# A perceiver block on one core: keys of 14 half batches by combined blocks, values as whole tiles, scores and weighted values two slots later

## The chip, the cores and the metric

One core of a Trainium2 chip runs the whole program. TensorE multiplies matrices into PSUM (8 banks of 512 f32 a partition), VectorE (DVE), ScalarE (ACT) and GpSimd (POOL) work elementwise, and SyncE (SP) issues transfers, transposes by DMA among them; POOL has no part in anything that lies in PSUM here. The engines run side by side and wait on semaphores. The metric is the device time in microseconds, the median of several executions.

## The reference

```python
def xattn(x, context, Wq, Wk, Wv, Wo, bo):          # 8 batches, 128 tokens of 512, context 2048 x 384
    q, k, v = x @ Wq, context @ Wk, context @ Wv     # 8 heads of 64
    sim = einsum('bihd,bjhd->bhij', q, k) * 64 ** -0.5
    return einsum('bhij,bjhd->bihd', softmax(sim), v) @ Wo + bo
x = x + xattn(layernorm(x), ctx_768, ...)
x = x + attn(layernorm(x), ...)    # causal, softmax over axis 1, with biases
x = x + ffn(layernorm(x), ...)     # 2048 hidden, relu, rounded to 8 bits
```

Nearly all the time is in the first line: keys and values of 8 x 2048 context rows.

## The kernel before

**Precision.** Each f32 operand is kept as a high and a low half in f16 (`_h`, `_l`; high by ScalarE, low = value minus high by VectorE or POOL), and a product is three passes: high x high, low x high, high x low (`three_passes`). So one block of keys, 128 features x 512 context rows with 384 summed, is 9 matmuls (3 passes, 3 pieces of 128).

**Slots.** The first stage is a loop over 128 slots, 16 a batch, 8 a half batch (1024 context rows). Slot s makes a key block (a pair p of heads, a quarter q of the rows; `key_quarter` into bank `k_ps`), a value step (`value_tiles`, two row tiles of 128 for half of the features, 2 x 9 matmuls of 256 columns into `v_ps`), and handles one head of one half batch: its scores (128 tokens x 1024 rows), its exponentials and its weighted values. Two heads of a pair, slots 2u and 2u+1, get their scores together (`scores(u)`, into banks `e_ps0` and `e_ps1`, 12 matmuls). A slot whose number modulo 16 is 8 or more is "behind": it works on the second half of its batch, so it has to join its maximum (`new_max`), its `fade` and its sum with those of the first half.

**Lags.** TensorE's slot s holds value step s+1, key block s, weighted values of slot s-5 (`PV_LAG`), and in even s the scores of unit s/2-1. VectorE takes the two maxima in the next odd slot. ScalarE (`steady`) takes the exponentials of slot s-3 (`X_LAG`) twice: `p_h` in f16, `p_f` in f32 with its sum. POOL makes `p_l` = `p_f` - `p_h` (`p_low`), SP transposes `p_h` and `p_l` by DMA to `pt_h` and `pt_l`, and TensorE waits for both in `weighted_values`, which uses banks `o_ps0` and `o_ps1` in turn; VectorE adds the result to `acc` (`accumulate`). Each engine's order is written out in code, and a wait holds up everything behind it on its engine.

**Beside it.** Once in four slots a quarter of the context (128 x 1536) is loaded into `raw` (2 buffers), its high half made by ScalarE (`ctx_high`), its low half by POOL (`ctx_low`). In slots whose number modulo 16 is 15, 1, 3 or 5, after a behind pair is done, POOL norms the output of a pair (`o_norm`, four instructions). In the last 16 slots the weights of later stages are split and turned. After the slots come projections, the second attention and the hidden layers (last, from about 750 us).

## Time and profile before

| what | value |
| --- | --- |
| median of 3 runs | 923.07 us (923.06 to 923.19) |
| the profiled execution | 923.73 us, of these 921.7 us from its first to its last instruction |
| granted clock of TensorE, mean | 0.997 |
| the 128 slots | from about 28 to about 715 us |
| TensorE busy | 905.2 us (98%) |
| VectorE, ScalarE, POOL busy | 548.3, 576.5, 507.4 us (59, 63, 55%) |

Matmuls overlap in the pipe, so the distance from one start to the next tells what one costs, not its own duration. A granted clock of 1.00 is the 2.4 GHz level. Idle time of an engine that nothing waits for costs nothing.

### The profile page before, as it was taken

How to read it: one execution, taken by the hardware profiler on the slowest of the kernel's cores; microseconds unless marked ns; L12 is line 12 of the kernel's file. 1: busy time of each engine (PE TensorE's matmuls, PEld its weight loads, DVE VectorE, ACT ScalarE, POOL GpSimd, SP SyncE). 2: the span in 40 equal slices, each digit the busy share in tenths (PEclk: the TensorE clock that was granted, in tenths of full speed). 3: DMA queues.
4: the chain of work that ended last, by engine and by line, in shares of the span. 5: the costliest groups of instructions: out<-in, count | busy, mean ns of one | idle time of the engine just before them, and what ended most of it. 6: DMA issues, size and time to landing. Idle time of an engine off the chain costs nothing.

```text
span 921.7 us, 19492 instructions
## 1 busy us (share of the span) xinstructions
PE 905.2 (98%) x7470; PEld 565.6 (61%) x7470; DVE 548.3 (59%) x973; ACT 576.5 (63%) x1014; POOL 507.4 (55%) x393
## 2 busy tenths in 40 slices
PE   7999999999999999999999999999999899999998
PEld 4556666666666666666666666666666455544444
DVE  6645565555555555655555565556667669886633
ACT  4756777776677777777776677777567423236540
POOL 4636567556555755675576556778876755310000
PEclk9999999999999999999999999999999999999999
DMA  9377576676657566565666666857997462223502
GB/s 339 84 150 161 138 132 136 159 142 144 144 132 139 127 144 142 128 143 140 139 153 144 143 138 141 198 132 149 182 189 157 92 127 70 71 85 74 183 12 81
DMA packets 340267, 126.35 MB, mean 137 GB/s; under 512 B 316112, under 2 KB 317904, under 8 KB 340176
## 3 DMA queue, kind: packets, MB, share of 16 engines
q1 hardware_dynamic: 324832, 95.87, 49.4%
q10 hardware_dynamic: 15344, 29.23, 10.6%
q8 instruction: 61, 1.00, 0.5%
q14 instruction: 30, 0.25, 0.1%
HBM read 45.36 MB, written 2.10 MB: 51 GB/s over the span
## 4 chain that ended last, share of the span: by engine, by line
PE 94%; ACT 2%; DVE 1%; DMA 1%; issue 1%; SPq 1%; ACTq 0%; DVEq 0%
PE v_ps L670 28%; PE k_ps L670 27%; PE e_ps L739 10%; PE e_ps L670 8%; PE o_ps L759 6%; PE o_ps L761 3%; PE e_ps L1021 3%; PE o_ps L776 2%; PE o_ps L1014 1%; PE e_ps L1014 1%; PE o_ps L954 1%; PE v_ps L1014 1%; SPq L636 1%; DMA raw<-in_ctx_t 1%; PE k_ps L1014 0%
## 5 line engine op out<-in xcount | busy, mean ns | idle before, releaser
L1979 POOL TENSOR_TENSOR p_l<-p_f,p_h 128x1024 f16<-128x1024 f32 x128 | 273.1, 2134 | 233.4 <-ACT p_f L1202 233.4
L1537 DVE TENSOR_REDUCE q_max<-e_ps 128x1 f32<-128x1024 f32 x128 | 153.4, 1219 | 48.9 <-PE e_ps L739 48.9
L1530 DVE TENSOR_TENSOR k_l<-k_ps,k_h 128x512 f16<-128x512 f32 x128 | 88.5, 691 | 126.3 <-ACT k_h L1166 126.3
L1523 DVE TENSOR_TENSOR v<-v_ps,v 128x512 f16<-128x512 f32 x127 | 87.8, 691 | 112.5 <-ACT v L1158 112.5
L1195 ACT ACTIVATE p_h<-e_ps,bias 128x1024 f16<-128x1024 f32 x128 | 143.3, 1120 | 2.4 <-issue 0.3
L1202 ACT ACTIVATE p_f<-e_ps,bias 128x1024 f32<-128x1024 f32 x128 | 142.1, 1111 | 0.0
L670 PE MATMUL v_ps<-wv_h,ctx_h 128*128 128x256 f16 x756 | 124.4, 273 | 1.7 <-DVE v L1523 1.7
L670 PE MATMUL v_ps<-wv_l,ctx_h 128*128 128x256 f16 x756 | 123.7, 273 | 0.0
L670 PE MATMUL v_ps<-wv_h,ctx_l 128*128 128x256 f16 x756 | 123.7, 273 | 0.0
L759 PE MATMUL o_ps<-v,pt_h 128*128 128x128 f16 x1024 | 104.2, 220 | 0.7 <-DVE acc L1554 0.7
L670 PE MATMUL k_ps<-ctx_h,wk_h 128*128 128x512 f16 x384 | 103.8, 379 | 0.0
L670 PE MATMUL k_ps<-ctx_h,wk_l 128*128 128x512 f16 x384 | 103.8, 379 | 0.0
L670 PE MATMUL k_ps<-ctx_l,wk_h 128*128 128x512 f16 x384 | 103.8, 379 | 0.0
L1969 POOL TENSOR_TENSOR ctx_l<-raw,ctx_h 128x1536 f16<-128x1536 f32 x31 | 96.1, 3099 | 13.4 <-ACT ctx_h L1145 11.7
L761 PE MATMUL o_ps<-v,pt_l 128*128 128x64 f16 x1024 | 100.8, 193 | 0.0
L759 PEld LDWEIGHTS o_ps<-v,pt_h 128*128 128x128 f16 x1024 | 90.3, 98 | 15.8 <-issue 0.9
L1158 ACT ACTIVATE v<-v_ps 128x512 f16<-128x512 f32 x127 | 75.0, 590 | 37.0 <-PE v_ps L670 35.0
L761 PEld LDWEIGHTS o_ps<-v,pt_l 128*128 128x128 f16 x1024 | 88.6, 98 | 15.0
L1166 ACT ACTIVATE k_h<-k_ps 128x512 f16<-128x512 f32 x128 | 76.6, 598 | 15.9 <-PE k_ps L670 15.7
L670 PEld LDWEIGHTS v_ps<-wv_h,ctx_h 128*128 128x128 f16 x756 | 64.6, 98 | 34.7 <-issue 28.5
L670 PEld LDWEIGHTS v_ps<-wv_h,ctx_l 128*128 128x128 f16 x756 | 74.0, 98 | 8.6
L670 PEld LDWEIGHTS v_ps<-wv_l,ctx_h 128*128 128x128 f16 x756 | 74.0, 98 | 8.6
(311 smaller groups left out, 1286.9 us busy)
## 6 DMA issues: line engine op xcount, KB each, us to landing
raw<-in_ctx_t ACTq DMA_DIRECT2D x27, 768.0 KB, 5.5
w_raw<-in_w_t SPq DMA_DIRECT2D x32, 256.0 KB, 4.0
raw<-in_ctx_t SPq DMA_DIRECT2D x4, 768.0 KB, 7.5
pt_h<-p_h SPq DMA_TRANSPOSE x128, 2.8
pt_l<-p_l SPq DMA_TRANSPOSE x128, 2.8
out<-xr SPq DMA_DIRECT2D x7, 256.0 KB, 2.0
x_in<-in_x SPq DMA_DIRECT2D x6, 256.0 KB, 8.4
o_all<-in_x ACTq DMA_DIRECT2D x6, 256.0 KB, 3.7
```

The source lines that it names most:

```text
L670: mm = pe.matmul(acc, a(c), m(c), start=(i == 0), stop=(i == len(todo) - 1))
L739: mm = pe.matmul(e_ps[h][:, i, :], left[rows, p, tokens], right[rows, u % K_RING, cols], start=first, stop=last)
L759: pe.matmul(acc_bank[:, 0:VW], pt_h[:, s % T_RING, j, :], v[g][:, tile, head, :], start=(j == 0), stop=False, skip_group_check=True)
L761: mm = pe.matmul(acc_bank[:, 0:DH], pt_l[:, s % T_RING, j, :], v[g][:, tile, head, 0:DH], start=False, stop=(j == 2 * JT - 1), skip_group_ ...
L1166: act.activation(k_h[:, u % K_RING, i * QW:i * QW + QW], k_ps[:, :], ACT.Copy).then_inc(k_hi, 1)
L1195: act.activation(p_h[:, s % H_RING, :, :], e_ps[s % 2][:, :, :], ACT.Exp, scale=EXP_SCALE, bias=bias[:, col:col + 1]).then_inc(p_hi, 1)
L1202: act.activation(p_f[:, s % F_RING, :, :], e_ps[s % 2][:, :, :], ACT.Exp, scale=EXP_SCALE, bias=bias[:, col:col + 1], accum_out=p_sum[:, c ...
L1523: dve.tensor_tensor(v[g][:, j0:j0 + 2, :, DH:VW], v_bank(s)[:, :].rearrange("p (j h d) -> p j h d", j=2, d=DH), v[g][:, j0:j0 + 2, :, 0:DH ...
L1530: dve.tensor_tensor(k_l[:, s // 2 % K_RING, cols], k_ps[:, :], k_h[:, s // 2 % K_RING, cols], ALU.subtract)\
L1537: ins = dve.tensor_reduce(q_max[:, col:col + 1], e_ps[s % 2][:, :, :].rearrange("p i n -> p (i n)"), AX, ALU.max, negate=True)
L1969: pool.tensor_tensor(ctx_l[b % 2][:, q, :, :], raw[:, i % 2, :, :], ctx_h[b % 2][:, q, :, :], ALU.subtract).then_inc(ctx_split, 1)
L1979: pool.tensor_tensor(p_l[:, s % L_RING, :, :], p_f[:, s % F_RING, :, :], p_h[:, s % H_RING, :, :], ALU.subtract).then_inc(p_split, 1)
```

## The change

**Keys.** For the half batches 1 to 14 (`mixed(s)`: slots 8 to 119) four slots make the four key blocks of two feature blocks and two quarters together. Of the three pieces of the sum, two form a 2 x 2 by 2 x 2 product of blocks, which is done with 7 products (Strassen) for 8; the third piece is added in plain. That is 33 matmuls of 512 columns for 36. The combined weights are made once (`key_weights` on POOL, `wk_high`, `wk_low`, 10 forms in `wf_h`, `wf_l`). The combined context blocks T1 to T4 are made once a half batch: POOL forms them in place in `raw` (`mix_ctx`, four instructions of 128x512), ScalarE their high halves (`mix_high`, two of 128x1024), POOL their low halves (`mix_low`, two). Sums of products that serve two results are copied by VectorE from PSUM to `kept` (`keep_product`, three a round of four slots) and added to a bank, into bank `s_ps` (`add_keys`, three a round); then ScalarE and VectorE split as before. `s_ps` is the bank that was `o_ps1` in the slots, so weighted values have `o_ps0` alone.

**Values.** From slot 8 on, a value step is one tile of 128 rows for all 512 features: 9 matmuls of 512 columns for 18 of 256.

**Order.** `X_LAG` 3 to 5, `PV_LAG` 5 to 7, scores of unit s/2-2 in even slots. In a round's slots 0 and 2 the weighted values stand first. Both quarters of a half batch's context are handled in its predecessor's slots 1 and 2 (modulo 8), mixes in 3 and 4, their splits in 5 and 6; `raw` has 3 buffers, the key ring 3 in place of 4. The work on the weights, the loads of x and the order after the slots are rewritten to fit. `bv_row` is loaded after the slots.

```diff
+        X_LAG, PV_LAG = 5, 7
...
+            return (s // 4, 2 * (s % 4), 2) if s < PER_HALF else (None, s % PER_BATCH, 1)
...
+                ctx_behind[at - 7], ctx_behind[at - 6] = 2 * hb, 2 * hb + 1
+                mix_behind[at - 5], mix_behind[at - 4] = (hb, 0), (hb, 1)
+                mixed_behind[at - 3], mixed_behind[at - 2] = (hb, 1), (hb, 0)
...
+            def key_product(s, acc, first, *terms):
...
+                key_product(s, s_ps, True, ("A12", (1, 0)), ("W0", (2, 0)))
...
+                key_product(s, k_ps, True, ("A11", (0, 0)))
+
+            def sixth_product(s):
+                pe.wait_ge(k_added, 3 * group_of(s) + 1)
+                pe.wait_ge(mix_split, mixed_at(s // PER_HALF, 0))
+                key_product(s, k_ps, False, ("S2", "T2"))
+
+            def fifth_product(s):
+                pe.wait_ge(k_split, split_at(group_of(s), 1))
+                key_product(s, s_ps, True, ("S1", "T1"), ("W1", (2, 1)))
+
+            def third_products(s):
+                pe.wait_ge(k_kept, 3 * group_of(s) + 3)
+                key_product(s, s_ps, False, ("S4", (1, 1)), ("WD", (2, 1)))
+                key_product(s, k_ps, False, ("S3", "T3"))
+
+            def fourth_product(s):
+                pe.wait_ge(k_added, 3 * group_of(s) + 3)
+                key_product(s, k_ps, False, ("A22", "T4"), ("W1", (2, 0)))
...
-                if s >= 2:
-                    pe.wait_ge(acc_ready, s - 1)
-                elif s == 0:
+                if s:
+                    pe.wait_ge(acc_ready, s)
+                else:
                     pe.wait_ge(q_split, 8)
-                acc_bank, head = o_ps[s % 2], 2 * (p % 2) + h
+                acc_bank, head = o_ps0, 2 * (p % 2) + h
...
+                j = s % 4 if mixed(s) else None
+                if j in (0, 2):
+                    weighted_values(s - PV_LAG)
                 if s + 1 < SLOTS:
                     value_tiles(s + 1)
...
+                elif j == 0:
+                    first_products(s)
+                elif j == 1:
+                    sixth_product(s)
                     weighted_values(s - PV_LAG)
+                    fifth_product(s)
+                elif j == 2:
+                    third_products(s)
+                else:
+                    weighted_values(s - PV_LAG)
+                    fourth_product(s)
+                if s % 2 == 0 and s >= 4:
+                    scores(s // 2 - 2)
...
+            weighted_values(SLOTS - 7)
+            scores(UNITS - 2)
+            fold(0)
+            weighted_values(SLOTS - 6)
+            project_out(0)
+            weighted_values(SLOTS - 5)
+            project_out(1)
             scores(UNITS - 1)
...
+                elif j == 0:
+                    v_high(s + 1)
+                    key_high(s, "C11")
+                elif j == 2:
+                    v_high(s + 1)
+                    key_high(s, "C12")
+                elif j == 3:
+                    key_high(s, "C21")
...
+                dve.tensor_copy(kept_sum[:, place_at, :], bank[:, :]).then_inc(k_kept, 1)
...
+                dve.tensor_tensor(s_ps[:, :], bank[:, :], other, ALU.add).then_inc(k_added, 1)
...
+                    keep_product(s, 2)
+                    keep_product(s, 3)
+                elif j == 2:
+                    gather(done)
+                    v_low(s + 1)
+                    add_keys(s, "C12")
+                    key_low(group_of(s), "C12")
+                    add_keys(s, "C22")
+                else:
+                    maxima(s)
+                    gather(done)
+                    v_low(s + 1)
+                    key_low(group_of(s), "C22")
...
+                    pool.tensor_tensor(left[:, 0, :], right[:, 0, :], left[:, 0, :], ALU.subtract).then_inc(mix_ready, 1)
...
                 if s in ctx_behind:
                     ctx_low(ctx_behind[s])
+                if s in mix_behind:
+                    mix_ctx(*mix_behind[s])
+                if s in mixed_behind:
+                    mix_low(*mixed_behind[s])
```

How the order changes on two engines. POOL, in the slots where an output is normed too (o_sum to o_half is `o_norm`, p_l a slot each, ctx_l a quarter of the context), before:

```order
L1995 TENSOR_TENSOR o_half<-o_f,o_half 128x128
L1979 TENSOR_TENSOR p_l<-p_f,p_h 128x1024
L1969 TENSOR_TENSOR ctx_l_87<-raw,ctx_h_86 128x1536
L1979 TENSOR_TENSOR p_l<-p_f,p_h 128x1024
L1986 TENSOR_TENSOR o_sum<-acc 128x128
L1989 TENSOR_TENSOR o_f<-o_sum,o_rec 128x128
L1993 CAST o_half<-o_f 128x128
L1995 TENSOR_TENSOR o_half<-o_f,o_half 128x128
L1979 TENSOR_TENSOR p_l<-p_f,p_h 128x1024 x2
```

POOL after the change, from slot 1 of an even half batch (raw<-raw is a mix):

```order
L2246 TENSOR_TENSOR ctx_l_93<-raw,ctx_h_92 128x1536
L2287 TENSOR_TENSOR p_l<-p_f,p_h 128x1024
L2246 TENSOR_TENSOR ctx_l_93<-raw,ctx_h_92 128x1536
L2287 TENSOR_TENSOR p_l<-p_f,p_h 128x1024
L2294 TENSOR_TENSOR o_sum<-acc 128x128
L2297 TENSOR_TENSOR o_f<-o_sum,o_rec 128x128
L2301 CAST o_half<-o_f 128x128
L2303 TENSOR_TENSOR o_half<-o_f,o_half 128x128
L2254 TENSOR_TENSOR raw<-raw 128x512
L2255 TENSOR_TENSOR raw<-raw 128x512
L2287 TENSOR_TENSOR p_l<-p_f,p_h 128x1024
L2258 TENSOR_TENSOR raw<-raw 128x512
```

The two ctx_l of a half batch now have one p_l between them, and mixes follow where there was p_l alone. VectorE, around the maxima (q_max) of a pair, before:

```order
L1537 TENSOR_REDUCE q_max<-e_ps 128x1 x2
L1566 TENSOR_SCALAR o_den<-p_sum,fade 128x1
L1554 SCALAR_TENSOR_TENSOR acc<-acc,fade,o_ps 128x128
L1571 RECIPROCAL o_rec<-o_den 128x2
L1523 TENSOR_TENSOR v_103<-v_ps,v_103 128x8x64
L1530 TENSOR_TENSOR k_l<-k_ps,k_h 128x512
```

And after, from the middle of slot 2 of a round to slot 3 (m_ps holds the banks k_ps and s_ps):

```order
L1761 TENSOR_TENSOR m_ps<-m_ps,kept 128x512
L1736 TENSOR_TENSOR k_l<-m_ps,k_h 128x512
L1761 TENSOR_TENSOR m_ps<-m_ps,kept 128x512
L1767 TENSOR_REDUCE q_max<-e_ps 128x1
L1772 TENSOR_SCALAR new_max<-q_max 128x1
L1767 TENSOR_REDUCE q_max<-e_ps 128x1
L1772 TENSOR_SCALAR new_max<-q_max 128x1
L1796 TENSOR_SCALAR o_den<-p_sum,fade 128x1
L1784 SCALAR_TENSOR_TENSOR acc<-acc,fade,o_ps 128x128
L1721 TENSOR_TENSOR v<-v_ps,v 128x2x4x64
```

Two sums and a low half of keys now stand ahead of the maxima, and the accumulation behind them.

## Rows read from the trace of the kernel before

**Rows 1.** The page: busy us, share of the span, instructions.
```profile
PE 905.2 (98%) x7470; PEld 565.6 (61%) x7470; DVE 548.3 (59%) x973; ACT 576.5 (63%) x1014; POOL 507.4 (55%) x393
```

**Rows 2.** Busy time by stretch: stretch, length, then PE, PEld, DVE, ACT, POOL, granted clock, DMA.
```profile
100.00:700.00 600.00, 600.00 (x5512) 402.57 (x5509) 344.71 (x601) 427.88 (x755) 388.47 (x270) 1.00 0.68 146
```

**Rows 3.** Timeline of TensorE: start, us, line, operation, out<-in, shapes, count.
```profile
303.40 0.39 PE L739 MATMUL e_ps<-k_h,q_h 64*128 64x512 f16 x2
...
304.80 0.50 PE L670 MATMUL v_ps<-wv_h,ctx_h 128*128 128x256 f16 x3
...
306.77 0.81 PE L670 MATMUL k_ps<-ctx_h,wk_h 128*128 128x512 f16 x3
307.42 0.81 PE L670 MATMUL k_ps<-ctx_h,wk_l 128*128 128x512 f16 x3
...
308.72 0.22 PE L759 MATMUL o_ps<-v,pt_h 128*128 128x128 f16 x1
...
309.40 0.49 PE L670 MATMUL v_ps<-wv_h,ctx_h 128*128 128x256 f16 x3
```

**Rows 4.** Timeline of POOL; in brackets idle before and who ended it.
```profile
301.06 0.45 POOL L1986 TENSOR_TENSOR o_sum<-acc 128x128 f32<-128x128 f32 x1
...
302.81 2.13 POOL L1979 TENSOR_TENSOR p_l<-p_f,p_h 128x1024 f16<-128x1024 f32 x1
...
309.27 2.13 POOL L1979 TENSOR_TENSOR p_l<-p_f,p_h 128x1024 f16<-128x1024 f32 x1 [1.12 <-ACT p_f L1202]
...
319.95 2.13 POOL L1979 TENSOR_TENSOR p_l<-p_f,p_h 128x1024 f16<-128x1024 f32 x1 [4.49 <-ACT p_f L1202]
```

**Rows 5.** Groups of POOL: busy us, mean ns; last, the landing of pt_l.
```profile
L1979 POOL TENSOR_TENSOR p_l<-p_f,p_h 128x1024 f16<-128x1024 f32 x128 | 273.1, 2134 | 233.4 <-ACT p_f L1202 233.4
L1969 POOL TENSOR_TENSOR ctx_l<-raw,ctx_h 128x1536 f16<-128x1536 f32 x31 | 96.1, 3099 | 13.4 <-ACT ctx_h L1145 11.7
...
L2075 POOL TENSOR_TENSOR xr<-xr,o_all 128x512 f32<-128x512 f32 x8 | 12.1, 1548 | 0.0
...
L2025 POOL TENSOR_TENSOR o_all<-o_all,bo_row 128x512 f32<-128x512 f32 x6 | 7.5, 1268 | 0.0
...
DMA to landing us min/median/max: 2.7/2.8/6.7
```

**Rows 6.** Timeline of all engines: rows of VectorE and ScalarE.
```profile
299.42 0.69 DVE L1530 TENSOR_TENSOR k_l<-k_ps,k_h 128x512 f16<-128x512 f32 x1 [0.89 <-ACT k_h L1166]
...
300.02 0.26 DVE L1566 TENSOR_SCALAR o_den<-p_sum,fade 128x1 f32<-128x1 f32 x1
...
300.21 0.33 DVE L1554 SCALAR_TENSOR_TENSOR acc<-acc,fade,o_ps 128x128 f32<-128x128 f32 x1
...
304.91 2.35 DVE L1537 TENSOR_REDUCE q_max<-e_ps 128x1 f32<-128x1024 f32 x2 [0.77 <-PE e_ps L739]
...
307.51 0.59 ACT L1158 ACTIVATE v<-v_ps 128x512 f16<-128x512 f32 x1
...
307.99 1.12 ACT L1202 ACTIVATE p_f<-e_ps,bias 128x1024 f32<-128x1024 f32 x1
```

**Rows 7.** Groups of ScalarE and VectorE: busy us, mean ns.
```profile
L1145 ACT ACTIVATE ctx_h<-raw 128x1536 f16<-128x1536 f32 x31 | 45.7, 1474 | 0.0
...
L1542 DVE TENSOR_SCALAR new_max<-q_max 128x1 f32<-128x1 f32 x64 | 13.7, 214 | 2.3
```

**Rows 8.** Timeline of TensorE after the last slot.
```profile
709.32 0.39 PE L739 MATMUL e_ps<-k_h,q_h 64*128 64x512 f16 x2
...
714.27 0.22 PE L759 MATMUL o_ps<-v,pt_h 128*128 128x128 f16 x1 [0.75 <-DVE acc L1554]
...
717.93 0.39 PE L739 MATMUL e_ps<-k_h,q_h 64*128 64x512 f16 x2 [2.82 <-ACT p_f L1202]
```

**Rows 9.** Busy time by stretch, there.
```profile
720.00:721.00 1.00, 1.00 (x4) 0.34 (x3) 0.96 (x3) 0.00 (x0) 1.00 (x1) 0.50 2.03 88
```

**Rows 10.** The chain of waits there: start, us, what.
```profile
719.57 4.17 PE v_ps L670 x12
```

More of the change, by code:

```diff
@@ L436, in made_bank @@
             return t_bank[(made.index(item) + 2) % 4]
[L438 removed]
+        fold_bank = [s_ps, s_ps, t_bank[0], t_bank[1]]
         def norm_at(what, r):
@@ new lines, in key_quarter @@
+                three_passes(k_ps[:, :], (lambda c: wh[c], lambda c: wl[c]),
+                             (lambda c: ch[:, q % 2, c, :], lambda c: cl[:, q % 2, c, :]), CC).then_inc(k_filled, 1)
+            def key_product(s, acc, first, *terms):
+                hb, c2 = s // PER_HALF, s % PER_HALF // 4
+                for part, (wi, xi) in enumerate(((0, 0), (1, 0), (0, 1))):
+                    for t, (name, block_of) in enumerate(terms):
+                        w = (wf_h, wf_l)[wi][:, FORMS.index(name), c2, :]
+                        if block_of in MIXES:
+                            x = (mix_h, mix_l)[xi][hb % 2][:, MIXES.index(block_of), :]
+                        else:
+                            x = (ctx_h, ctx_l)[xi][hb % 2][:, block_of[1], block_of[0], :]
+                        mm = pe.matmul(acc[:, :], w, x, start=(first and part == 0 and t == 0),
+                                       stop=(part == 2 and t == len(terms) - 1), skip_group_check=True)
+                mm.then_inc(k_filled, 1)
@@ L1214, in _ @@
             k_high(0)
-            wk_high(slice(P, D))
+            for n in range(1, 4):
+                wk_high(n)
             ctx_high(1)
@@ L1549, in accumulate @@
                 dve.wait_ge(pv_done, s + 1)
-                new, total = o_ps[s % 2][:, 0:VW], acc[:, p, h, :]
+                new, total = o_ps0[:, 0:VW], acc[:, p, h, :]
                 if half:
@@ L1600, in _, with gather, maxima @@
                 q_low(i)
-            def steady(s):
-                done = s - PV_LAG - 1
-                if s % 2 == 1 and 0 <= s - X_LAG < SLOTS:
+            def gather(done):
+                if behind(done):
+                    add_sums(done)
+                accumulate(done)
+                if stage_end(done) is not None:
+                    o_reciprocal(stage_end(done))
+            def maxima(s):
+                slot_maximum(s - X_LAG)
+                slot_maximum(s - X_LAG + 1)
@@ L1606, in steady @@
                     slot_maximum(s - X_LAG)
+                    key_low(group_of(s), "C11")
                     slot_maximum(s - X_LAG + 1)
[L1609 to L1618 removed]
```

553 lines of the change are left out of this document (365 added, 188 removed).

## Prediction, made before the changed kernel ran

> **What bounds the kernel now.** I read first the busy time of each engine over the whole span, and the same in the stretch from 100 to 700 us [rows 1, 2]. TensorE is busy 905.2 of 921.7 us, and for all 600.00 us of that stretch, at a granted clock of 1.00 (the 2.4 GHz level). So in the slots TensorE sets the pace, and a saving there is worth its full size until another engine fails to deliver in time. POOL (GpSimd) is busy 388.47 of those 600 us, VectorE 344.71, ScalarE 427.88: there is room on average.
>
> Then the timeline of TensorE over one pair of slots [rows 3]: scores take 303.40 to 304.80, a value step (18 matmuls of 256 columns) to 306.77, so 1.97 us, a key step (9 of 512 columns) to 308.72, so 1.95 us, 0.65 per three, and weighted values to 309.40, 0.68 us. POOL's p_l instructions of even slots start at 309.27 and 319.95 [rows 4]: two slots last 10.68 us, four 21.36, a half batch (8 slots) 42.72.
>
> **What TensorE saves.** In each of 28 rounds of four slots the keys need 33 matmuls for 36: three fewer, 0.65 us. A whole value tile is 9 matmuls of 512 columns, by the key step's spacing 9 x 0.216 = 1.94 against 1.97, so 0.03 a slot, 0.1 a round. A round becomes 21.36 - 0.75 = 20.6 us, a half batch 41.2. Over 28 rounds that is 21.0 us; the 8 plain slots at the end add 0.2. Unhindered the median 923.1 would become 901.9.
>
> The TensorE page of the Trainium skill ("TensorE: Matmul & The Clock Gate", Back-to-back issue gap) gives a sustained spacing of 131 ns for 512 columns, beside 2.5 ns plus the columns for an isolated one. By the sustained figure the whole tiles alone would take 9 x 0.131 = 1.18 us a slot and some 90 us would go. The trace does not agree: matmuls of just this shape, back to back, are 0.216 apart [rows 3].
>
> **A round after the change, on TensorE's own clock** (0 = start of the round, no waits; 0.1 between scores and their neighbours). Slot 0: weighted values 0 to 0.7, value 2.6, two products into s_ps 3.9, one into k_ps 4.6, scores 4.7 to 6.0. Slot 1: value 6.1 to 8.0, sixth product 8.7, weighted values 9.3, fifth 10.6. Slot 2: weighted values 11.3, value 13.3, third products 14.6 (s_ps) and 15.2, scores 15.3 to 16.6. Slot 3: value 16.7 to 18.6, weighted values 19.3, fourth 20.6. Two things now stand at a slot's start that stood at its end: the weighted values of slots 0 and 2. They need (a) the transpose of p_l and (b), since there is one bank o_ps0 for two, VectorE's accumulation of the step before.
>
> **What is added elsewhere.** POOL, per half batch: four mixes of 128x512 in f32, no such row. The nearest are 1.27 us for o_all with bo_row and 1.55 for xr with o_all [rows 5]; I take 1.30, as the first is the nearest in kind (both inputs large, VectorE busy beside it); ends 1.2 and 1.55. Two low halves of 128x1024, 2.1 us each by p_l. Together 9.4 us. VectorE, per round: three copies out of a bank and three sums of a bank and SBUF, 128x512; k_l of the same size takes 0.69 with 0.60 from start to start [rows 6], so 3.9 us; VectorE stood at 57% of 21.36, so 12.3, and comes to 16.2 of 20.6 (79%). ScalarE: two of 128x1024 a half batch, 1.0 each (two thirds of ctx_h's 1.47 [rows 7]). Loads of the context stay 768 KB each, with three buffers for two: I cost them at nothing.
>
> The GPSIMD page of the skill ("GPSIMD Engine Reference", The C++ chunk loop) states a floor of about 2.5 cycles an element for two inputs. Worked out at its clock that would be an estimated 1.07 us for a mix; the sum below would then be some 6 us lower in all. The rows of 128x512 stand above it [rows 5].
>
> **POOL in the even half batches.** There every second slot also has o_norm, four instructions, 301.06 to 302.81 = 1.75 us [rows 4]. Averages hide the place: count from the scores of slot 0 in a half. VectorE's first maximum starts 1.51 after scores start (303.40, 304.91 [rows 3, 6]), so at 6.2. These slots also take new_max (0.21 and about 0.04 for the wait [rows 7]), and key_low of C11 (0.60) lies between the maxima: 6.2 + 1.18 + 0.25 + 0.60 + 1.18 + 0.25 = 9.65, p_f starts at 9.85 and p_l can start 1.28 later (307.99, 309.27 [rows 4, 6]), at 11.1. From there POOL has without a pause: p_l of slots 1 to 6, 6 x 2.09 = 12.5; o_norm of 1, 3, 5, 5.25; two ctx_l, 6.2 [rows 5]; four mixes, 5.2; the first mix_low, 2.1: 31.3 us. Its last p_l ends at 42.4, and its transpose lands 2.7 later [rows 5], at 45.2. TensorE wants it at 41.2. Each p_f is ready before POOL gets to it (the tightest, slot 5, by 0.8). So an even half lasts about 45.2: TensorE waits 4.0 us in it. By intermediate sums the waits are 2.4 us at slot 4 (p_l of slot 2 starts at 18.1, behind o_norm and ctx_l, instead of 14.8; lands 23.0, wanted 20.6), 1.0 at slot 6, 0.6 at the end. Before, the same p_l landed with ample time: weighted values stood at the end of the second slot behind it.
>
> **VectorE in the odd half batches.** No o_norm there, so POOL delivers within about 0.2. But the end of a round is a chain: in slot 1 p_f, fade and mix_high end on ScalarE at 12.1, p_h, p_f and v of slot 2 at 14.8 (p_f takes 1.12 and p_h has its size, each about 1.05 to the next start, v 0.6 [rows 6]); v_low 15.4; sum C12 16.1; its high half 16.75, low half 17.5; sum C22 18.2; two maxima with new_max 21.0; then o_den and acc, 0.53 [rows 6]: 21.5, where the next weighted values want it at 20.6. That is 1.0 in the second round; in the first round (ctx_high 1.47, but no new_max nor fade) 0.2. Odd halves: 41.2 + 1.2 = 42.4. In the even halves the same chain would cost 1.5 at slot 4, hidden under POOL's 2.4.
>
> **The sum.** Even halves 45.2 - 42.7 = +2.5, seven of them +17.5; odd ones 42.4 - 42.7 = -0.3, seven -2.1; plain slots -0.2. The tail: the last scores wait for p_f now, 8.6 us after the scores before them (709.32, 717.93), with 0.75 and 2.82 us of idle [rows 8] and a granted clock of 0.50 behind it [rows 9]. After the change the last but one wait so, and the last have cover: 1.3 of scores, three sets of 12 matmuls (2.6 each) and two weighted values, 10.5 us. The start, with scores a slot pair later, may lose an early wait. I take 0 for both, ends -4 and +3. Profiled span 921.7 + 15.2 = 936.9; what lies around it (923.73 - 921.7 = 2.0) stays; the median is 0.7 below the profiled execution: 923.1 + 15.2 = **938.3 us**.
>
> **Rivals.** (1) *TensorE stays the bound*: POOL's chain lags less than its rows say, or the p_l order gives enough room. Against it: 31.3 us of POOL work, for which 41.2 - 11.1 - 2.7 = 27.4 are there. For it: latencies are tenths, and all depends on differences. With a fifth to nothing of the waits it gives 902 to 909; with half, 920. Faster, 0.25. (2) *The clock falls*: the idle of 2.4 us at slot 4 of even halves could do what the tail shows, where 0.75 and 2.82 us of idle with 0.7 of work between them brought a granted clock of 0.50 (the 1.2 GHz level) [rows 8, 9]. Each time costs about 1.6 us (twelve matmuls in 4.17 [rows 10], for 12 x 0.216 = 2.6), seven 11: 949. It decides only if 2.4 us of idle suffice, which no row shows. 0.15. (3) *ScalarE and VectorE become the bound everywhere*: p_f of slot 0 is ready 0.4 before scores want it (25.3); if the sums into a bank cost 0.3 more each, every round is 0.6 longer: 28 x 0.6 on top, 955. 0.08. (4) *Nothing to tell*: waits just eat the 21 us, 923. 0.05. The forecast itself, waits of 28 to 45 us in all, has 0.47: 930 to 947.
>
> **Chances and range.** This kernel can be told from no change at 0.2% (1.8 us). Faster 0.25 (rival 1), same 0.05 (rival 4), slower 0.70. The mix price moves 7 x 4 x 0.25 = 7 us, p_f of slot 1 another 3, the tail 4. From 908 to 950 no more than 2 in 10 is left out (the best part of rival 1, rival 3 and the worst of rival 2).
>
> **What would show it.** TensorE idle before weighted values (o_ps<-v,pt_h), some 35 us in all where there is 0.7 now, released by a DMA (pt_l) in even half batches and by VectorE's acc in odd ones; key and value rows near 0.216 a matmul; POOL without a gap from the second to the seventh slot of an even half and a mix at 1.3 us; even half batches of 45, odd ones of 42.4. Wrong at the first step, if TensorE is still 99% busy in the slots; wrong at the POOL step, if its waits in both kinds of half are alike; at the chain step, if scores wait for p_f; rival 2, if the granted clock falls in the middle.

## The result, and the profile after

| | before | after |
|---|---|---|
| median of the runs, us | 923.13 (923.06 to 923.42) | 985.63 (982.33 to 987.2) |
| profiled execution, us | 923.73 | 985.50 |
| its span, us | 921.7 | 983.7 |
| scores of slot 8 start at, us | 79.1 | 85.1 |
| from there to the scores of slot 120 | 598.2 | 634.5 |
| from there to the end | 244.4 | 264.0 |

The ratio is 1.0672, interval 1.0644 to 1.0699: 6.7% slower. Slower was forecast, but at 938.3 us, with a range that ended at 950. The three last lines of the table share out the 62 us: 6.0 at the start, 36.3 in the slots, 19.6 in the tail. The forecast was 0, 15.4 (less 0.2 in the plain slots) and 0. The two ends are not quite like for like: slot 8 now has the scores of a unit earlier, so one set of scores and two weighted values, by [rows 3] an estimated 2.8 us of TensorE's work, have passed from the start to the tail. With that counted back the start lost 8.8 us and the tail 16.8.

The page of the changed kernel, as in [rows 1]: TensorE has 1164 matmuls less (6306 for 7470), is busy as long as before and has a lower share of a longer span.
```profile
PE 907.9 (92%) x6306; PEld 448.8 (46%) x6306; DVE 653.3 (66%) x1143; ACT 602.4 (61%) x1046; POOL 639.8 (65%) x482
```
The stretch of [rows 2], the same columns: TensorE 560.37 of 600 us in place of all of it, at a granted clock of 0.98 on average.
```profile
100.00:700.00 600.00, 560.37 (x4141) 273.51 (x4140) 408.14 (x719) 430.24 (x743) 470.03 (x321) 0.98 0.62 136
```
What TensorE waited for from 85 to 720 us (line, who released it, us in all, times, the longest). Before, this view has no row for the slots.
```profile
PE o_ps L902 <- issue: 23.3, 14, 2.9
PE o_ps L902 <- DMA pt_l<-p_l: 14.9, 7, 2.2
PE o_ps L902 <- DVE acc L1784: 1.3, 8, 0.2
PE v_ps L764 <- DVE v L1721: 1.0, 1, 1.0
```
40.5 us, nearly all before weighted values, as forecast (some 35). But few of them are released by VectorE. "issue" means that the view names no releaser; these stand at slot 6 of a half batch (one at slot 2). The trace can still tell what they are. Each of the 14 ends 0.09 us behind the landing of a pt_l, that is the start of the transpose plus its time to landing. For the wait that ends at 202.69 (a row shown below) the one transpose issued between 196 and 200 us is
```profile
L681 SPq DMA_TRANSPOSE pt_l<-p_l x1: 1233/1233/1233, 197.5 to 197.5; - x1
...
DMA to landing us min/median/max: 5.1/5.1/5.1
```
so TensorE waits here for a transpose that is slow to land; the experiment with the load tells why it is slow.

POOL's groups of the changed kernel, for [rows 5]:
```profile
L2287 POOL TENSOR_TENSOR p_l<-p_f,p_h 128x1024 f16<-128x1024 f32 x128 | 273.9, 2140 | 133.1 <-ACT p_f L1384 130.3 <-DMA pt_l<-p_l 2.4
L2246 POOL TENSOR_TENSOR ctx_l<-raw,ctx_h 128x1536 f16<-128x1536 f32 x31 | 96.1, 3100 | 12.8 <-ACT ctx_h L1309 12.7
L2265 POOL TENSOR_TENSOR mix_l<-raw,mix_h 128x1024 f16<-128x1024 f32 x28 | 60.1, 2145 | 21.9 <-ACT mix_h L1316 21.9
L2258 POOL TENSOR_TENSOR raw<-raw 128x512 f32<-128x512 f32 x14 | 17.8, 1268 | 0.1
```
The mix costs 1.27 us where 1.30 was taken, its low half 2.15 where 2.1 was.

A half batch took 42.7 us before. After, from scores to scores: even ones 44.9, 44.9, 47.7, 47.7, 44.9, 45.0, 47.4 (forecast 45.2), odd ones 43.2, 46.0, 43.9, 43.2, 43.3, 45.9, 46.4 (forecast 42.4). So the even ones that nothing else disturbed came as forecast, and the excess is in the odd ones and in single halves of 46 and more. These hold the second surprise, the clock. TensorE behind one of the longer idles, and then two stretches there (columns as in [rows 2]):
```profile
202.69 0.26 PE L902 MATMUL o_ps<-v,pt_h 128*128 128x128 f16 x1 [2.41 <-issue]
203.94 1.47 PE L764 MATMUL v_ps<-wv_h,ctx_h 128*128 128x512 f16 x3
```
```profile
202.00:204.00 2.00, 1.31 (x17) 1.34 (x18) 0.00 (x0) 1.66 (x3) 2.00 (x2) 0.66 0.59 116
204.00:206.00 2.00, 2.00 (x7) 0.66 (x6) 0.29 (x1) 0.00 (x0) 2.00 (x2) 0.50 0.98 223
```
After an idle of 2.41 us three matmuls take 1.47 us from first to last end where 0.81 was usual [rows 3], at the 1.2 GHz level. Six such falls lie between slots 8 and 120, near 203, 340, 418, 566, 657 and 691 us. Busy time times what was missing of the clock, summed over stretches of 2 us, is 9.2 us, 1.5 each; rival 2 had put 1.6 on one. The same sum gives 4.0 us between 20 us and the scores of slot 8 (falls near 66 and 76 us) and 4.4 from slot 120 on, where the kernel before has 0 and 1.7. So some 16 of the 62 us are lost clock, 4.0 of them at the start and 2.7 in the tail.

### The profile page after: what moved, and what is told of

Its sections match the earlier page's. It is cut to its first block, busy times and chain, and to the rows that moved or that the text cites. A ratio compares the mean times of both kernels' runs of the same rounds, so it can differ in the third digit from the quotient of the medians.

```text
span 983.7 us, 17461 instructions
## 1 busy us (share of the span) xinstructions
PE 907.9 (92%) x6306; PEld 448.8 (46%) x6306; DVE 653.3 (66%) x1143; ACT 602.4 (61%) x1046; POOL 639.8 (65%) x482
## 3 DMA queue, kind: packets, MB, share of 16 engines
q1 hardware_dynamic: 324432, 95.09, 44.9%
## 4 chain that ended last, share of the span: by engine, by line
PE 71%; DVE 9%; issue 6%; POOL 6%; ACT 4%; DMA 3%; SPq 1%; ACTq 0%; DVEq 0%; POOLq 0%
PE v_ps L764 21%; PE m_ps L832 15%; PE e_ps L764 7%; PE e_ps L882 6%; PE o_ps L902 5%; DVE q_max L1767 4%; PE m_ps L764 3%; PE e_ps L1176 3%; POOL p_l L2287 3%; PE o_ps L904 2%; DMA pt_l<-p_l 2%; POOL ctx_l L2246 2%; PE e_ps L1169 1%; DVE m_ps L1761 1%; PE m_ps L1169 1%
## 5 line engine op out<-in xcount | busy, mean ns | idle before, releaser
L1348 ACT ACTIVATE k_h<-m_ps 128x512 f16<-128x512 f32 x112 | 66.7, 596 | 108.5 <-DVE m_ps L1761 108.4
L764 PE MATMUL v_ps<-wv_h,ctx_h 128*128 128x512 f16 (+1 forms) x396 | 108.1, 383 | 1.5 <-DVE v L1721 1.5
L764 PE MATMUL v_ps<-wv_h,ctx_l 128*128 128x512 f16 (+1 forms) x396 | 106.9, 380 | 0.0
L764 PE MATMUL v_ps<-wv_l,ctx_h 128*128 128x512 f16 (+1 forms) x396 | 104.7, 374 | 0.0
L2246 POOL TENSOR_TENSOR ctx_l<-raw,ctx_h 128x1536 f16<-128x1536 f32 x31 | 96.1, 3100 | 12.8 <-ACT ctx_h L1309 12.7
L1736 DVE TENSOR_TENSOR k_l<-m_ps,k_h 128x512 f16<-128x512 f32 x112 | 76.8, 686 | 36.1 <-ACT k_h L1348 36.1
L1743 DVE COPY kept<-m_ps 128x512 f32<-128x512 f32 x84 | 55.2, 685 | 56.0 <-PE m_ps L832 56.0
L2265 POOL TENSOR_TENSOR mix_l<-raw,mix_h 128x1024 f16<-128x1024 f32 x28 | 60.1, 2145 | 21.9 <-ACT mix_h L1316 21.9
L832 PE MATMUL m_ps<-ctx_h,wf_h 128*128 128x512 f16 x196 | 65.4, 380 | 0.0
L832 PE MATMUL m_ps<-ctx_l,wf_h 128*128 128x512 f16 x196 | 65.2, 379 | 0.0
L832 PE MATMUL m_ps<-ctx_h,wf_l 128*128 128x512 f16 x196 | 65.1, 379 | 0.0
```

Of the source, the lines that this page charges most:

```text
L764: mm = pe.matmul(acc, a(c), m(c), start=(i == 0), stop=(i == len(todo) - 1))
L832: mm = pe.matmul(acc[:, :], w, x, start=(first and part == 0 and t == 0), stop=(part == 2 and t == len(terms) - 1), skip_group_check=True)
L1736: dve.tensor_tensor(k_l[:, u, cols], src[:, :], k_h[:, u, cols], ALU.subtract).then_inc(k_split, 1)
L2246: pool.tensor_tensor(ctx_l[hb % 2][:, i % 2, :, :], raw_of(i), ctx_h[hb % 2][:, i % 2, :, :], ALU.subtract).then_inc(ctx_split, 1)
```

## Experiments

All twelve kernels are variants of the changed one. The times from scores to scores are read from TensorE's timeline, each from the one profiled execution of its kernel; how much they scatter was not measured.

| kernel | median us | ratio to before (interval) | slots 8 to 120 | to the end |
|---|---|---|---|---|
| changed kernel | 985.6 | 1.0672 (1.0644 to 1.0699) | 634.5 | 264.0 |
| e1_load_late | 970.4 | 1.0512 (1.048 to 1.0543) | 621.0 | 264.4 |
| e2_norm_late | 979.0 | 1.0603 (1.0587 to 1.0619) | 629.4 | 262.1 |
| e3_tail_spread | 988.8 | 1.0726 (1.0695 to 1.0756) | 633.6 | 265.0 |
| e4_plain_keys | 945.0 | 1.0232 (1.0217 to 1.0247) | 598.4 | 264.8 |
| e5_ends | 979.8 | 1.056 (1.0483 to 1.0637) | 640.0 | 254.8 |
| e6_middle | 960.9 | 1.0422 (1.0371 to 1.0474) | 611.1 | 262.2 |
| e7_all | 951.2 | 1.03 (1.028 to 1.0319) | 610.4 | 257.2 |
| e8_gather | 975.6 | 1.0553 (1.0519 to 1.0587) | 627.1 | 262.2 |
| e9_keeps_short | 961.1 | 1.0412 (1.0397 to 1.0428) | 609.1 | 265.3 |
| e10_mixes_short | 968.7 | 1.0502 (1.0477 to 1.0526) | 619.7 | 262.3 |
| e11_share | 958.0 | 1.0381 (1.0351 to 1.0411) | 616.8 | 259.0 |
| e12_order | 954.3 | 1.0348 (1.0331 to 1.0365) | 614.3 | 255.4 |

**A load beside a transpose.** e1_load_late moves one DMA by one slot:
```
             if hb > 1:
-                load_behind[at - 12], load_behind[at - 9] = 2 * hb, 2 * hb + 1
+                load_behind[at - 11], load_behind[at - 9] = 2 * hb, 2 * hb + 1
```


> The changed kernel with one edit: the first context load of each half batch is issued by ScalarE one slot later (slot 5 of a half batch in place of slot 4). Theory A (the 768 KB load runs beside the transpose of p_l that the weighted values of slot 6 need, which lands after 3.8 to 5.1 us in place of 2.7): TensorE's idle of 0.9 to 2.9 us at slot 6 of the odd half batches falls below 0.4, some 12 us in all, and the falls of the granted clock behind the idles of 2.4 us and more go with it, 2 to 3 us each for three or four of them: 963 to 970 us. Theory B (VectorE's or POOL's chain is late there and the load only stands beside it): nothing moves, 984 to 987. Theory C (the load now meets another needed transpose): the idle moves to slot 0 of the next half batch and the time stays within 3 us.

Measured 970.4, 15.2 less. The changed kernel has this at slot 4 of a first (odd) half batch (timeline: start, us, queue or engine; then, from the view of the tile pt_l, how long the one transpose issued from 108 to 112 us took to land):
```profile
107.23 0.37 ACTq L1415 DMA_DIRECT2D raw<-in_ctx_t  x1
...
109.12 1.23 SPq L681 DMA_TRANSPOSE pt_l<-p_l  x1
...
113.34 0.22 PE L902 MATMUL o_ps<-v,pt_h 128*128 128x128 f16 x1 [1.37 <-issue]
```
```profile
DMA to landing us min/median/max: 4.1/4.1/4.1
```
and e1_load_late, with the load a slot later (the same two views, the landing for 109 to 112 us):
```profile
110.37 1.23 SPq L681 DMA_TRANSPOSE pt_l<-p_l  x1
...
112.09 0.40 ACTq L1415 DMA_DIRECT2D raw<-in_ctx_t  x1
...
113.25 0.22 PE L902 MATMUL o_ps<-v,pt_h 128*128 128x128 f16 x1
```
```profile
DMA to landing us min/median/max: 2.8/2.8/2.8
```
(All of e1_load_late is 1.3 us later here, so its 113.25 is on time.) The transpose beside the load lands after 4.1 us and the weighted values of slot 6 start 4.2 behind its issue, after a wait; without the load it lands after 2.8 and nothing waits. Slow landings are not new: between slots 8 and 120 the kernel before has them up to 6.7 us and e4_plain_keys up to 6.5, and in neither does TensorE wait for one. There the weighted values stand at the end of a slot. The Trainium skill ("Trainium Kernel Development and Optimization", Key Constraints) says that DMAs issued from different engines' queues all run on the same 16 DMA engines and interleave; by that rule a load on ScalarE's queue can hold up a transpose on SP's, and these rows agree. Odd half batches fell to 42.1 to 42.5 us, all but one: theory A, and the forecast's 42.4 with it. The one left, 48.2, has the loads of x (slots 104 to 111) in it: TensorE waits 3.6 us for a pt_l that took 6.3 to land, and the clock falls behind that. Whether the loads of x are the cause isn't shown: e7_all, where they stand in other slots, has 42.6 there, but so has e6_middle, where they stand as here (a wait of 0.8 us).

**POOL's order.** e2_norm_late takes o_norm of batches 0 to 4 out of the slots in which it stands ahead of ctx_l (the transposes of its result stand a slot later with it):
```
+            NORM_BEHIND[PER_BATCH * b + (21 + p if b < 5 else 17 + 2 * p)] = n
...
-                done = s - PV_LAG - 1
-                if done >= 0 and stage_end(done) is not None:
-                    o_norm(stage_end(done))
...
+                if s in NORM_BEHIND:
+                    o_norm(NORM_BEHIND[s])
```


> The changed kernel with one edit: POOL's o_norm of batches 0 to 4 stands at slots 5, 6, 7 and 8 behind the batch's end in place of slots 1, 3, 5 and 7, behind the slot's other POOL work; the amount of work is the same. Theory A (POOL's order makes the p_l of the even slots late in the even half batches): their idles of 2.1 us and 1.0 at slots 4 and 6 go, five even half batches fall from 44.9 to 47.7 us to about 42, the odd ones stay: 12 us of waits and two falls of the clock at 2.7, so 966 to 972 us. Theory B (those waits come from the DMA side, loads and transposes, and not from POOL's order): 983 to 987 us.

Measured 979.0, 6.6 less. The wait at slot 4 of an even half changed its kind and size: 2.1 us for the transpose of p_l before, now
```profile
145.26 0.22 PE L907 MATMUL o_ps<-v,pt_h 128*128 128x128 f16 x1 [1.13 <-DVE acc L1789]
```
That is the VectorE wait which the prediction had at 1.5 us, hidden under POOL's 2.4. Theory A for the cause of the wait at slot 4; the time lies between the two theories. Slot 6 of the even halves went on waiting, 1.0 to 2.6 us, for transposes that met the load. TensorE was idle for no less of the slots than before, 42.2 us for 41.0; what this run gained there, 5.1 us, goes with the clock, which fell twice in place of six times. Together the two edits gave 24.7 us, where their sum is 21.8:

> The changed kernel with the edits of e1_load_late and e2_norm_late together. Alone they gave 15.2 and 6.6 us. Theory A (two causes, and in e2_norm_late the load's transfer still made slot 6 wait, now in the even half batches too): together they give more than the sum: odd half batches 42.2 us, the even ones with moved o_norm about 42.5 (1.1 of wait for VectorE's accumulation left), no fall of the clock in them; slots 8 to 120 take 602 to 608 us against 634.5, and the time is 952 to 960. Theory B (the two are independent): 963 to 965. Theory C (one cause, both take away the same waits): 968 or more.

Measured 960.9, just above theory A's 952 to 960 and below B's 963: even halves with a moved o_norm 43.3 to 43.8, odd ones 42.2 to 43.7, and no fall of the clock in them, as A had it. Its four executions lie between 958.7 and 968.3, so the 2.9 us beyond the sum are not shown by the times; the wait at slot 6 of the even halves, gone now, is what speaks for A.

**Without the combined products.** e4_plain_keys has `mixed(s)` return False and no mixes:
```
         def mixed(s):
-            return PER_HALF <= s < SLOTS - PER_HALF
+            return False
```


> The changed kernel without the combined products: the keys of all slots by 36 plain products a round, no mixes, no kept products or sums; whole value tiles, the two later slots, one bank for the weighted values, three buffers of raw context and the moved work of the tail stay. Theory A (TensorE sets the pace again as soon as POOL's mixes and VectorE's sums are gone): slots 8 to 120 at 21.26 us a round, 28 rounds 595 us against 634.5, so 39 less, with the start's 6 and the tail's 19.6 us still there: 944 to 950 us. Theory B (the later slots and the one bank cost by themselves, by waits on the accumulation): TensorE idles before weighted values of every round, over 0.2 us each, and the time is above 952. Theory C (start and tail were late because of the combined products' work too): below 940.

Measured 945.0: theory A. Its stretch from 100 to 670 us, and all that TensorE waited for from slot 8 to 120:
```profile
100.00:670.00 570.00, 568.21 (x4274) 288.82 (x4272) 324.18 (x571) 405.74 (x720) 356.46 (x247) 1.00 0.66 145
```
```profile
PE e_ps L880 <- ACT p_f L1382: 1.8, 7, 0.3
```
So the two later slots, the one bank and the whole tiles cost the slots nothing: 598.4 us against 598.2. (Two slots take 10.64 us against 10.68, the 0.02 a slot that whole tiles give; seven waits of 0.25 for p_f take back most of it.) The combined products, meant to save TensorE 21 us, cost 36.1 with the order that belongs to them: where `mixed(s)` is false the weighted values stand at the slot's end again, so this kernel doesn't tell the products from their order. The start is 79.2 us, as before the change, so the 6.0 us there come with the combined products; the tail, 264.8 us, is long without them too.

**The amounts.** Two kernels cut work out of the suspected engines.

> e6_middle with VectorE's three kept copies of a round cut to 64 of 512 columns from the second round on (so most of the keys that need them are computed from stale sums); everything else runs. Each copy is then some 0.5 us shorter, 1.5 of VectorE's round. Theory A (with loads and POOL's order mended, VectorE's chain is what keeps a round above TensorE's 20.6 us): odd half batches fall from 42.2 to 43.7 to about 41.4, even ones from 43.4 to 42 to 42.5, slots 8 to 120 from 611 to 595 to 600, 945 to 950 us in all. Theory B (POOL and the transposes set what is left): odd ones stay at 42.2 or more, 958 to 962.

Measured 961.1, the same as e6_middle: theory B by its numbers. VectorE's chain in e9_keeps_short, rows of a second round:
```profile
201.62 0.69 DVE L1767 TENSOR_TENSOR m_ps<-m_ps,kept 128x512 f32<-128x512 f32 x1
202.97 0.69 DVE L1741 TENSOR_TENSOR k_l<-m_ps,k_h 128x512 f16<-128x512 f32 x1 [0.66 <-ACT k_h L1353]
203.77 0.70 DVE L1767 TENSOR_TENSOR m_ps<-m_ps,kept 128x512 f32<-128x512 f32 x1
204.38 1.22 DVE L1773 TENSOR_REDUCE q_max<-e_ps 128x1 f32<-128x1024 f32 x1
...
205.76 1.21 DVE L1773 TENSOR_REDUCE q_max<-e_ps 128x1 f32<-128x1024 f32 x1
...
207.32 0.34 DVE L1790 SCALAR_TENSOR_TENSOR acc<-acc,fade,o_ps 128x128 f32<-128x128 f32 x1
```
The kept copies lie ahead of an idle of VectorE and are not in this chain, which begins with the third product's sum; the accumulation ends at 207.66 and a second round takes 21.49 us whether the copies are long or short. A round wants 20.63 to 20.7. So in the odd half batches it is VectorE that is late, by what stands behind the copies, and not POOL as B had it; in the even ones the second round (21.46) waits for a pt_l that landed in the usual 2.7 to 2.8 us, so there p_l itself comes late.

> e1_load_late with POOL's four mixes of a half batch cut to 64 of 512 columns (so the mixes are wrong in the other columns); o_norm stays in its old slots. POOL has some 4.3 us less in each half batch. Theory A (in the even half batches TensorE waits for POOL's 31.3 us between its second and its last p_l, as the prediction worked out): the idles of 2.1 us at slot 4 and about 1 in all behind it go, and VectorE's 1.1 to 1.5 us at slot 4, hidden till now, comes up: even half batches of 42.3 to 43 in place of 45, odd ones at 42.2 as before; slots 8 to 120 in 602 to 608 us, 951 to 958 in all. Theory B (the transposes are late for another reason than POOL's order): even ones at 44.5 or more, 967 to 971.

Measured 968.7, 1.7 less than e1_load_late: theory B by the time. But A's mechanism was only half tried. The waits, slots 8 to 120:
```profile
PE o_ps L902 <- DMA pt_l<-p_l: 15.2, 7, 2.4
PE o_ps L902 <- issue: 8.7, 9, 3.0
```
The seven waits of 2.1 us are for the p_l at slot 2, which stands behind o_norm and ctx_l and ahead of all mixes. I had overlooked in that expectation what the prediction itself says. What the mixes do delay, the p_l behind them, brought 0.5 us in an even half batch (its second round 21.47 us for 21.99); and five even half batches had a fall of the clock, four of them behind their 2.1 us, where e1_load_late had three.

**Another order on VectorE and ScalarE.**

> e1_load_late with one more edit: in each fourth slot VectorE accumulates the weighted values between the two maxima, in place of behind both. Theory A (what is left of waits in the odd half batches, 0.5 to 0.7 us a half before the weighted values of a round's first slot, is VectorE's accumulation in line behind the maxima): these waits go, seven times 0.6, 4 us: 965 to 967 against 970.4; the even half batches stay at 45. Theory B (the second maximum, 0.6 us later, makes p_f and with it p_l later): the even ones grow by about 0.6 each, the sum is the same, 969 to 972.

> e7_all without the accumulation between the maxima, and with the first kept copy of a round on ScalarE (0.6 us) in place of VectorE. Theory A (VectorE is the bound of what is left and ScalarE has room): half batches of 42 to 42.6, slots 8 to 120 in 596 to 602 us with the two late even half batches at 45, start at 80.4, 257 us from slot 120 on: 936 to 944. Theory B (ScalarE's chain from p_h to p_f is as tight; the copy makes p_f late and scores wait for it): idle before scores in each round, 950 or more.

> e7_all with the same work and another order in each mixed round: in the fourth slot VectorE does the first maximum, the accumulation, the low half of the value tile and then the second maximum (e7_all had the value's low half behind the second maximum), in the third slot ScalarE copies the value tile ahead of p_f; besides, o_norm of batches 5 and 6 is moved like that of the others. Theory A (what holds a second round at 21.5 us is the chain forecast: third product, sum C12, its high and low half, sum C22, two maxima, and whatever stands behind them, the accumulation in e6_middle, the value's low half in e7_all, in each case 0.5 to 0.7 us late): with both ahead of the second maximum the waits of 0.4 to 0.6 us at the end of a second round and for v go, a half batch is 41.5 to 42.2 us in both kinds, slots 8 to 120 take 586 to 596, the whole 925 to 938. Theory B (something behind the second maximum is late in its turn: C22's low half or p_h, and with it p_l on POOL): half batches stay at 42.5 or more, 942 to 952.

e8_gather gave 975.6, e11_share 958.0, e12_order 954.3: none is faster than the kernel it was made from (970.4, and for the last two 951.2). What TensorE waited for in the slots of e8_gather, and in those of e12_order:
```profile
PE v_ps L764 <- DVE v L1721: 6.4, 13, 1.7
```
```profile
PE o_ps L917 <- issue: 18.5, 30, 2.2
PE e_ps L897 <- ACT p_f L1399: 7.8, 15, 0.8
```
In e8_gather the waits for the accumulation are gone and 13 for v are there; odd half batches 42.6 in place of 42.2. In e12_order both are gone: scores wait for p_f in 15 places, up to 0.8 us, and the 30 waits of "issue" end, like those above, 0.09 us behind the landing of a pt_l. One of them, and the transpose issued between 151 and 153 us:
```profile
154.06 0.22 PE L917 MATMUL o_ps<-v,pt_h 128*128 128x128 f16 x1 [0.53 <-issue]
```
```profile
L694 SPq DMA_TRANSPOSE pt_l<-p_l x1: 1232/1232/1232, 151.2 to 151.2; - x1
...
DMA to landing us min/median/max: 2.7/2.7/2.7
```
18 of the 30 landed so, in 2.7 to 2.8 us, as quick as any: there p_l itself came late. In e11_share the waits for the accumulation are longer (12.8 us in 13 places; 0.96 at the end of most second rounds of odd half batches, up to 0.70 in e6_middle, where the accumulation also stands behind both maxima); ScalarE's copy is the likely cause, but e11_share also lacks e7_all's place for the accumulation. Theory B in e12_order by mechanism, at 954 against its 952; in e8_gather neither, since the time is above both and the even half batches didn't grow by 0.6 each; in e11_share a third thing, neither waits for scores nor a gain. Each order hands the 0.5 to 0.8 us of a second round to another reader. e12_order has no fall of the clock between slots 8 and 120 and is at 614.3 us there all the same.

**Start and tail.** e3_tail_spread and e5_ends:

> The changed kernel with one edit: the eight pairs of weight transposes stand one behind each of the slots 115 to 122 on SP's queue, in place of 1, 2, 1, 2, 1 and 1 behind 115, 117, 118, 119, 120 and 121. Theory A (the pairs that stand two together delay the transposes of p_h and p_l, for which TensorE waits 1.5 + 0.6 + 3.7 + 3.8 us in the last slots): 5 to 8 us less, 978 to 981. Theory B (the queue is full from 739 to 776 us whatever the order, so that the same sum is only shared out in another way): within 2 us of the changed kernel, 984 to 987.

> The changed kernel with two edits, one before slot 8 and one behind slot 112, which the trace tells apart. At the start VectorE's two low halves of the combined key weights (2.2 us each) stand behind the maxima of slot 7 in place of ahead of them. At the end the turned aq weights get a home of their own in the mixes' buffer that is idle from slot 112 on, so that their transposes start at slot 112 and not at 115 (the norms of rows 4 to 7 move to another buffer, and two sets of products change places for it). Theory A (start: TensorE waits 2.75 and 3.73 us for a chain behind these two low halves; end: the transposes of the weights, held back until the context of slot 119 is used up, fill SP's queue from 739 to 776 us and with it delay p_l): the scores of slot 8 start 3 to 4.4 us earlier, and from the scores of slot 120 to the end it takes 246 to 252 us in place of 264: 963 to 970 us in all. Theory B (the queue is as full with four slots more, and the order of folds costs as much): the end stays above 258, 978 to 983.

e3_tail_spread gave 988.8, no less than the changed kernel (the intervals overlap): theory B. SP's queue of the changed kernel shows why; this is a part of what is back to back from 739 to 776 us:
```profile
739.09 1.30 SPq L667 DMA_TRANSPOSE aq_h<-av_h  x1
740.43 1.27 SPq L667 DMA_TRANSPOSE aq_l<-av_l  x1
741.75 1.27 SPq L667 DMA_TRANSPOSE aq_h<-av_h  x1
743.05 1.90 SPq L667 DMA_TRANSPOSE aq_l<-av_l  x1
745.06 1.25 SPq L678 DMA_TRANSPOSE pt_h<-p_h  x1
746.35 1.31 SPq L681 DMA_TRANSPOSE pt_l<-p_l  x1
747.71 1.27 SPq L667 DMA_TRANSPOSE aq_h<-av_h  x1
```
Sixteen transposes of weights, 1.3 us each, have to pass with those of p, 14 of them here. What TensorE waited for from 720 us to the end, in the changed kernel, and, for e5_ends, from 723 us:
```profile
PE o_ps L902 <- issue: 6.8, 5, 3.7
PE o_ps L902 <- DMA pt_l<-p_l: 3.8, 1, 3.8
PE v_ps L764 <- DMA q_l<-o_half: 3.3, 1, 3.3
PE o_ps L902 <- DVE acc L1784: 1.6, 1, 1.6
```
```profile
PE o_ps L912 <- DVE acc L1798: 5.3, 2, 3.6
PE e_ps L774 <- DMA at_l<-n_half: 1.4, 1, 1.4
```
The main edits of e5_ends:
```
-        WEIGHT_BEHIND = {115: (0,), 117: (1, 2), 118: (3,), 119: (4, 5), 120: (6,), 121: (7,)}
+        WEIGHT_BEHIND = {112: (0,), 113: (1,), 114: (2,), 115: (3,), 117: (4,), 118: (5,), 120: (6,), 121: (7,)}
...
-                if i == 0:
-                    sp.wait_ge(k_filled, last_keys(SLOTS - PER_HALF - 1))
+                if i in (0, 4):
+                    sp.wait_ge(k_filled, last_keys(SLOTS - (1 if i else 2) * PER_HALF - 1))
...
-                elif s == 6:
-                    wk_low(4)
-                    wk_low(5)
```
(the two `wk_low` stand behind the maxima of slot 7 instead). From slot 120 on it took 254.8 us in place of 264.0, and the start 1.7 us less (4.8 in e7_all, where also the load of slot 4 is a slot later; the wait there is for the accumulation, behind VectorE's queue, 1.2 to 5.0 us in these kernels). Between A and B at both ends: the earlier home is worth 9.2 of the tail's 19.6 us, less than A had. What replaced the waits for transposes is VectorE's accumulation, 3.6 us in one place, which the single bank lets through to TensorE. The slots took 5.5 us longer than in the changed kernel. 2.5 of these lie in the last half batch (49.9 for 47.4), into which transposes of weights have moved, but e6_middle has 49.9 there without that; the rest lies in half batches that no edit of e5_ends touches. Of its four executions one took 966.4 us (mean granted clock 0.989) and three 979.4 to 981.1 (0.981 to 0.984). Waits that hang on where a load and a transpose meet, and the falls behind them, may differ so from execution to execution; with one trace it isn't shown. The times of the regions are read beside the medians for that reason, and a difference of a few us in one region is weak evidence by itself.

**All together.**

> The changed kernel with the edits of e5_ends and e6_middle, VectorE's accumulation between the two maxima of each fourth slot in place of behind them, and the loads of x in other slots (97, 99, 101, 103, 105, 107, 111, 115 for 104 to 111). Theory A (with the causes named, TensorE is the bound again): half batches of 41.3 to 42 us, two of 45 left, slots 8 to 120 in 586 to 594 us, start 81.5, from slot 120 on 246 to 252: 915 to 927 us, about the kernel before, from 2 behind it to 8 ahead. Theory B (POOL at 36 to 39 of 41 us in every half batch leaves no room, and waits come back in other slots): slots 8 to 120 stay above 600, 930 or more.

Measured 951.2: 34 us less than the changed kernel, and theory B on the slots (610.4 us). Its odd half batches take 42.5 to 43.3, the even ones 43.3 to 43.7 with two of 46.0 and 47.9. No version beats the kernel before.

## Why the prediction was right and wrong

**The first step** (TensorE's saving) held: a round without a wait takes 20.7 us (10.64 and 10.05 in e1_load_late), against 20.6, so it saves 0.67 us a round where 0.75 was counted. The 131 ns that the Trainium skill states for a matmul of 512 columns ("TensorE: Matmul & The Clock Gate", Back-to-back issue gap) have no support in the runs either: the two slots of e4_plain_keys take 10.64 us.

**The POOL step** held for what it described: 44.9 against 45.2 us an undisturbed even half batch, waits of 2.1 and 1.0 at slots 4 and 6 against 2.4 and 1.0, the first one released by the transpose of p_l, and with o_norm moved replaced by a wait of 1.1 us for VectorE. (The 1.0 was right in part by chance: without the load beside it, in e1_load_late, it is 0.6.) Mix prices of 1.27 for 1.30. The Trainium skill's floor of 2.5 cycles ("GPSIMD Engine Reference", The C++ chunk loop), which by an estimate made 1.07 us of a mix, is not reached by the mixes. By the same estimate p_l (128x1024) would take 2.13 and ctx_l (128x1536) 3.20; they take 2.14 and 3.10, so the longer instructions stand at that figure or just under it, and only the short mixes take clearly more an element.

**The VectorE chain** held, but it was hidden by something else. The forecast's 1.2 us an odd half batch, 42.4, is what e1_load_late shows in six of seven (42.1 to 42.5), with 0.5 to 0.7 of it as a wait for acc where 1.0 was forecast; that the total comes so near is in part luck, since the rounds themselves take 0.1 more than 20.6. e2_norm_late and e9_keeps_short confirm two details: 1.1 us come up at slot 4 when POOL's 2.1 go, and the kept copies are not in the chain.

**The step that failed first** is "Loads of the context stay 768 KB each ...: I cost them at nothing". Their size did stay. But the change moved the issue of the first one from slot 3 to slot 4 of a half batch and took away the slack behind the transpose that it now meets: before, a late p_l had time till the end of its slot, now weighted values stand at the slot's start. The view to ask was in the rows: the landing of pt_l, 2.7 at the least, 2.8 in the median and 6.7 at the most [rows 5]; the sum used 2.7 for every one, where the slow end of that row had become the price. Measured, the transposes before slot 6 took 3.1 to 6.1 us, and moving the load away gave 13.5 us in the slots (634.5 to 621.0) with the falls that followed.

**The second** is rival 2, left out of the forecast with 0.15: the clock did fall, six times between slots 8 and 120 at 1.5 us, 9.2 us together, against seven at 1.6. Its condition, "only if 2.4 us of idle suffice", was met by idles of 2.2 to 2.9 us, though not by all: in e1_load_late two idles of the same kind, 2.15 and 2.17 us, were followed by a clock of 0.75 and of 1.00 (stretches of 2 us behind them, columns as in [rows 2]):
```profile
234.00:236.00 2.00, 2.00 (x21) 1.16 (x22) 1.20 (x4) 2.00 (x4) 2.00 (x2) 0.75 0.42 95
147.00:149.00 2.00, 2.00 (x23) 1.23 (x22) 1.20 (x4) 2.00 (x4) 2.00 (x2) 1.00 0.33 73
```
It was no rival but an addition to the forecast's own waits.

**The third**, and by its size the largest, is "I take 0 for both, ends -4 and +3" for start and tail: 6.0 and 19.6, of the 46.9 us beyond the forecast. The tail's sum looked at TensorE's cover for the last scores, and not at SP's queue. The diff had the rows for it: the transposes of weights begin at 115 in place of 111 and stand two together, since their home is now the context of slot 119. Sixteen at 1.3 us are 21 us of a queue which p_l has to pass. Of the 19.6 us 13.1 are more idle time of TensorE (21.1 for 8.0), 2.7 more lost clock and an estimated 2.8 the work that passed over from the start. At the start TensorE waits 2.8 us for p_f and 3.7 for the accumulation, and 4.0 us of clock are lost beside these waits. The two low halves of combined weights (2.2 us each on VectorE) lay ahead of the maxima; I had counted work per round and none for the weights' own. Moving them gave 1.7 us, so they are a part of it; e4_plain_keys shows that the rest also comes with the combined products.

**The sum**, then: 15.2 forecast, plus 10.6 (odd half batches beyond 42.4, without their three falls: mostly the loads), 9.2 (clock) and 1.5 (even ones beyond 45.2, without theirs) in the slots, plus 6.0 and 19.6 at the ends is 62.1; the span moved by 62.0. The mechanism of the forecast was there and had its size. The range was too narrow because costs put at nothing had no upper end, or one of 3 us, and rival 2, which adds to the forecast, was priced as if it stood in its place.

**Open**: why one idle of 2.1 us is followed by a fall and another is not; why half batch 13 of e1_load_late takes 48.2 us and that of e6_middle 42.6; what each of the waits that e5_ends left in the tail comes from (13.4 us of idle, 3.6 of it one wait for the accumulation); and whether a layout with two banks for weighted values beside the combined products would hold 20.7 us a round. It wasn't tried.

## What to carry over

When a change takes the slack from behind a transfer, price that transfer by the slowest landing in its row and list each DMA, on any queue, that is now issued within a few us of it. Where work of one buffer is moved, follow what next uses that buffer up to the end of the program: here the place chosen for the turned weights delayed their transposes by four slots, and an earlier one gave back 9.2 us of the tail. And when a saving on the bound engine is small beside the chains of the others (0.65 us a round here), remove the change's mechanism in one run first: e4_plain_keys told in one kernel that it cost 36 us, with its order, where it was meant to give 21. When a view names no releaser for a wait, compare the end of the wait with the landings of what it could need: that takes no run.

## What the runs showed of the hardware

- A transpose of 256 KB of p_l by DMA, 2.8 us from issue to landing, took 4.1 beside a load of 768 KB from another queue (up to 6.1 in the slots, and up to 6.7 in the kernel before).
- 14 waits of TensorE in the changed kernel, and 30 in e12_order, for which the view names no releaser, each end 0.09 us behind the landing of the transpose that they need.
- Six falls of the granted clock to the 1.2 GHz level behind idles of 2.2 to 2.9 us, 1.5 us each, in the midst of a stretch at 93% busy; two more before slot 8, at waits of 2.8 and 3.7 us. Not every such idle brings one (2.28 us at 432 us brought none). e12_order, whose slots have one idle above 1.6 us (2.19), has none there.
- Two executions of one kernel differed by up to 14.6 us (e5_ends), with a mean granted clock of 0.989 in the fastest and 0.981 in the slowest; the kernel before, run beside it, stays within 3.2. The cause isn't shown.
